# A vision-transformer step pipelined over 128 images: score units in another order, the keys' placement signalled in two halves, and new orders on all engines

## What is computed

```python
h = layernorm(layernorm(patches) @ W + b)          # tok: embedding, PD = 768 -> D = 192
a = layernorm(h)                                    # causal attention, 12 heads of 16
q, k, v = split(a @ w_attn + b_attn)
s = (q*scale) @ k.T + (q*scale) @ rel.T             # relative term by key position
h = h + softmax(where(causal, s, -inf)) @ v @ w_proj + b_proj
hid = layernorm(h); n = layernorm(hid)*g1 + b1      # routed block: 29 tokens of 196
score = sigmoid(n @ Wr + br); idx = the 29 lowest   # these get full attention, 12 heads
merged = where(idx, attention(n) @ Wo + bo, (n + score*pooled) @ Wm + bm)
h3 = hid + merged
out = h + h3 + gelu(layernorm(h3) @ W1 + bf1) @ W2 + bf2
```

## Time and profile before

| what | value |
|---|---|
| time, median of 3 runs | 4944.79 us (4944.5 to 4948.51) |
| the profiled execution's own time | 4944.02 us |
| its span, first to last instruction | 4942.2 us |
| mean granted TensorE clock | 0.989 of full speed |
| busy share of the span: PE / weight loads / DVE / ACT / POOL | 95 / 87 / 78 / 70 / 62 % |

### The profile page before, as it was taken

One profiled execution on the slowest core, in us unless ns is written; L12 is line 12 of the kernel. 1 busy time (PEld: TensorE's weight loads), 2 busy tenths in 40 slices (PEclk: granted clock), 3 DMA queues, 4 the chain that ended last, 5 costly groups with the idle time before them and its releaser, 6 DMA issues. The chain is left out here.

```text
span 4942.2 us, 143405 instructions
## 1 busy us (share of the span) xinstructions
PE 4696.2 (95%) x44376; PEld 4299.3 (87%) x44376; DVE 3872.3 (78%) x13015; ACT 3448.9 (70%) x12030; POOL 3065.9 (62%) x4143
## 2 busy tenths in 40 slices
PE   3899999999999999999999999999999999999998
PEld 3788888888888888888888888888888888888887
DVE  3787887887888788788788878878878877887885
ACT  1667777776776777777677677777777767767775
POOL 2566666666666666666666666666666666666664
PEclk7899999999999999999999999999999999999999
DMA  5555555455555555555555555555554555555551
GB/s 70 68 68 72 69 71 72 66 74 67 69 73 67 72 70 70 72 67 73 69 67 74 67 70 72 68 72 69 71 71 66 74 67 69 72 67 72 70 70 21
DMA packets 339085, 340.16 MB, mean 69 GB/s; under 512 B 47652, under 2 KB 306033, under 8 KB 339057
## 3 DMA queue, kind: packets, MB, share of 16 engines
q1 hardware_dynamic: 332522, 337.37, 52.3%
q10 hardware_dynamic: 6535, 2.45, 0.3%
HBM read 204.78 MB, written 19.27 MB: 45 GB/s over the span
## 5 line engine op out<-in xcount | busy, mean ns | idle before, releaser
L1610 ACT ACTIVATE p<-banks,negmax 98x98 f32<-98x98 f32 (+1 forms) x3072 | 1139.3, 379 | 216.9 <-issue 121.8
L544 POOL TENSOR_TENSOR p<-p,rden 98x392 f32<-98x392 f32 x1152 | 980.9, 870 | 280.8 <-DVE rden L1242 280.7
L1226 DVE TENSOR_REDUCE negmax<-banks 98x2 f32<-98x392 f32 (+1 forms) x1152 | 609.6, 557 | 141.0 <-PE banks L732 122.2
L732 PE MATMUL banks<-kz,qparts 128*98 128x392 f32 x2304 | 648.9, 385 | 0.0
L1610 ACT ACTIVATION_READ_ACCUMULATOR p<-banks,negmax 98x1 f32 x3072 | 612.0, 199 | 0.0
L743 PE MATMUL banks<-tokw,x_sb 128*98 128x193 f32 x3072 | 592.4, 336 | 15.5 <-POOLq L556 14.6
L743 PEld LDWEIGHTS banks<-tokw,x_sb 128*98 128x98 f32 x3072 | 553.9, 252 | 20.3 <-issue 14.6
L767 PE MATMUL banks<-ident,p 98*98 98x98 f32 x4608 | 530.4, 252 | 24.1 <-ACTq L1614 4.1
L695 PE MATMUL banks<-z3Ts,w_split 128*128 128x196 f32 x3840 | 508.4, 279 | 33.7 <-ACT gT L1685 32.3
L695 PEld LDWEIGHTS banks<-z3Ts,w_split 128*128 128x128 f32 x3840 | 468.2, 192 | 64.2 <-ACT gT L1685 58.0
L535 POOL TENSOR_TENSOR gparts<-gT,gparts 128x392 fp32r<-128x392 f32 x384 | 395.2, 1040 | 190.9 <-DVE gparts L1434 190.9
(11 more groups left out here) (264 smaller groups left out, 11542.3 us busy)
## 6 DMA issues: line engine op xcount, KB each, us to landing
x_sb<-in_x SPq DMA_DIRECT2D x384, 196.0 KB, 5.0
kz<-kq SPq DMA_DIRECT2D x1024, 73.5 KB, 2.6
x_sb<-in_x SPq DMA_DIRECT2D x256, 190.8 KB, 8.9
x_sb<-in_x SPq DMA_DIRECT2D x256, 185.5 KB, 11.1
qparts<-kq SPq DMA_DIRECT2D x256, 147.0 KB, 2.7
x_sb<-in_x SPq DMA_DIRECT2D x128, 189.0 KB, 7.3
out<-out_row SPq DMA_DIRECT2D x128, 147.0 KB
pT<-in_L_ffn_W ACTq DMA_DIRECT2D x1, 576.0 KB
```

Source lines behind the costliest of these rows:

```text
L544: gp.tensor_tensor(heads, heads, rden[:, g, t, s0:s0 + sn].unsqueeze(2).broadcast_to([HT, sn, w]), ALU.mult).then_inc(sem["pnorm_sb"], 1)
L732: last = mm(o, qparts[:, g, HT * t:HT * t + HT], kz[:, slots[0]:slots[-1] + 1, part, g, 0:w], start=False, stop=part == 1, skip_group_chec ...
L1226: ve.tensor_reduce(negmax[:, g, t, slots[0]:slots[-1] + 1], bank[RING[f"S{k}"]][0:HT, 0:w * len(slots)].rearrange("p (s w) -> p s w", w=w) ...
L1610: sc.activation((p1 if t else p0)[0:HT, 4 * g + s], bank[b][0:HT, w * i:w * i + w], ACT.Exp, bias=negmax[:, g, t, s:s + 1], accum_out=den[ ...
```

## The change

1. `s_unit`: in each group the unit of the last rows' heads 0 and 1 is scored first, then the one of all four heads' first rows, then that of heads 2 and 3. Each unit's work is the same as before.
2. `place_keys`: the two `qparts` copies are issued first; the eight `kz` copies are signalled by two semaphores, `kza_in` (slots 0 and 1) and `kzb_in` (slots 2 and 3). S0 waits for `q_in` and `kza_in`, S1 for `kzb_in`.
3. The lists of `step` on PE, DVE, ACT and POOL are ordered anew. No instruction is added or dropped, except that the changed lists split or join waits.

The core of the diff, with hunks of the same kind left out ("..."):

```diff
-    g, part = divmod(u, 3)
+    g, j = divmod(u, 3)
+    part = (1, 0, 2)[j]
...
                 sp.wait_ge(sem["kqlo_sb"], after("kqlo_sb", n))
+                for part in range(2):
+                    sp.dma_start(qparts[64 * part:64 * part + 64].bitcast(F32),
+                                 kq[64:128, part].bitcast(F32)).then_inc(sem["q_in"], 16)
...
-                                         sem["kz_in"], 16)
-                for part in range(2):
-                    sp.dma_start(qparts[64 * part:64 * part + 64].bitcast(F32),
-                                 kq[64:128, part].bitcast(F32)).then_inc(sem["q_in"], 16)
+                                         sem["kza_in" if s < 2 else "kzb_in"], 16)
...
-                            pe.wait_ge(sem["kz_in"], after("kz_in", n))
+                            pe.wait_ge(sem["kza_in"], after("kza_in", n))
+                        if k == 1:
+                            pe.wait_ge(sem["kzb_in"], after("kzb_in", n))
```

More of the change, by code:

```diff
@@ L67 @@
 SEMS = dict(
-    x_in=len(XROWS) * 16, out_done=16, kz_in=8 * 16, q_in=2 * 16,
+    x_in=len(XROWS) * 16, out_done=16, kza_in=4 * 16, kzb_in=4 * 16, q_in=2 * 16,
     tok_mm=1, sqs_mm=1, zT_mm=1, score_mm=1, mrow_mm=1, usum_mm=1, kk_mm=1, vv_mm=1, aT_mm=1, kq_mm=1, v_mm=1,
@@ L593, in step @@
                 if front:
[L594 to L597, removed]
                     normalised(8)
+                if back:
+                    gp.drain()
+                    gp.tensor_tensor(h2b[:], h2[:], both(bf2), ALU.add).then_inc(sem["h2b_sb"], 1)
                 if head:
@@ L619, in step @@
                         sem["f_rstd"], 1)
+                if tail:
+                    gelu_low(2)
+                if back:
+                    gp.wait_ge(sem["h3_stat"], after("h3_stat", m))
+                    rstd(mv_3[:, :, 1], ve5[:], rstd5[:], "h3_rstd")
                 if back:
@@ L992, in step @@
                 if back:
+                    score()
                     keys2()
[L994 to L999, removed]
                 if front:
                     causal("S0")
+                if back:
+                    values2()
+                    mixing_rows()
+                if front:
                     causal("S1")
@@ L1051, in step @@
                     up(2)
+                if front:
+                    attention()
+                if head:
+                    attention_cols()
                 if back:
                     attn_out()
-                if head:
-                    attention_cols()
-                if front:
-                    attention()
-                if back:
-                    scatter()
                 if front:
@@ L1063, in step @@
                     keys()
+                if back:
+                    scatter()
                 if tail:
@@ L1464, in step @@
                     sigmoid()
+                if front:
+                    maxima(0)
+                if back:
                     mixing_rows()
                 if front:
-                    maxima(0)
                     maxima(1)
-                    maxima(2)
-                if tail:
-                    mlp_cols_lo()
-                if front:
-                    maxima(3)
                 if back:
@@ L1477, in step @@
                     inverse_sums(0)
-                    inverse_sums(1)
+                    maxima(2)
+                    maxima(3)
                 if back:
@@ L1481, in step @@
                 if front:
-                    inverse_sums(2)
+                    inverse_sums(1)
                     maxima(4)
                     maxima(5)
+                if back:
+                    q_blocks()
+                if front:
+                    inverse_sums(2)
+                if tail:
+                    mlp_cols_lo()
+                if front:
                     inverse_sums(3)
@@ L1487, in step @@
                 if back:
-                    q_blocks()
+                    max2()
+                if front:
+                    inverse_sums(4)
+                    maxima(7)
+                    inverse_sums(5)
                 if head:
@@ L1502, in step @@
                 if front:
-                    maxima(8)
+                    transposed("A0")
                     inverse_sums(6)
-                    transposed("A0")
                 if head:
-                    embedding_scaled()
+                    embedding()
                 if front:
@@ L1521, in step @@
                     attention_input()
+                if front:
+                    attention()
+                if head:
+                    attention_cols_lo()
                 if tail:
@@ L1524, in step @@
                     gelu_parts(1)
+                if front:
+                    residual()
                 if back:
                     attn_out()
[L1527 to L1528 removed]
                 if tail:
                     gelu_parts(2)
[L1531 to L1532 removed]
+                if head:
+                    keys()
                 if back:
@@ L1692, in step @@
                     values()
+                if tail:
+                    mlp_cols_hi()
+                if front:
                     load_table(ACT.Exp)
@@ L1721, in step @@
                     softmax(8)
+                if tail:
+                    load_table(ACT.Gelu)
+                if front:
                     transposed("A1")
@@ L1727, in step @@
                 if tail:
-                    load_table(ACT.Gelu)
                     gelu(0)
```

86 lines of the change are left out of this document (31 added, 55 removed).

## The result

The changed kernel takes 4861.7 us (median of 3 runs, 4861.03 to 4862.09) against 4944.79 us: 83 us less. The ratio of the runs is 0.983, with a 95% interval of 0.9807 to 0.9852. The forecast was 4830 (4775 to 4900), faster.

A forecast was written before the change was run, and what follows sets the result against it. PE bounds the kernel, with 2.30 us of waits in each 37.40 us body. 25.0+11.3 gave 36.3, 37.40-2.30+1.58 gave 36.68; 36.5 was taken, saving 112 over 124 bodies and about 3 elsewhere: 4830 us (4775 to 4900).

The forecast's parts named there:

- (b): On PE, A1 and B0 take 1.07 where eight transposes need 0.70: 0.37 us of waiting per body.
- (c): On PE, A2 and A3 up to `context2` take 1.15 for 0.70: 0.45 us of waiting per body.
- (d): On PE, B1, A4, A5, B2 and the wait of up(2) take 2.11 for 1.40: 0.71 us per body.
- (e): On PE, `scatter` to `projection` takes 0.83 where 0.36 is needed: 0.47 us of waiting behind DVE's yparts.
- new wait of 0.35 for qb: PE could reach `scores2` before the routed block's queries are ready: 0.35 us of new waiting per body.
- h1b and h2b on POOL: These moved POOL operations lie beside work of other engines and were priced at nothing.
- the 6.84 of the sum: On PE, up(2), attention, attention_cols, attn_out, projection and keys together take 6.84 us at full pace.
- late a_row: Rival, chance 0.18: POOL products hold `embedding_scaled` and the h1 write, 0.3 each; period 37.0, 4895 us.
- those 2.30 us: Five listed waits inside PE per body, the only source of gain besides smaller waits.
- Slower: Rival, chance 0.08: DVE operations held up beside POOL make `ao` 1.3 later; period 37.8, 4995 us.
- No difference: Rival, chance 0.04: ACT's chain starts no earlier, since nTs comes as much later as S0 earlier; 4945 us.
- Better: Rival, chance 0.10: `ao` and gelu_low(2) find DVE and POOL earlier; period 35.9, 4760 us.

The follow-up runs named there:

- e2b: Changed kernel with `place_keys` as before: eight `kz` copies, then `qparts`, one semaphore that S0 waits for; 5301.4 us, ratio 1.0717.
- e11: Kernel before with the changed lists of all four engines from up(2) on; 5014.0 us, ratio 1.0131 to the kernel before.
- e3b: Changed kernel with POOL's h2b moved back ahead of `normalised(0)`; 4833.2 us, ratio 0.9769 to the kernel before.
- e9: Changed kernel with all four lists as before from up(2) on; 5144.7 us, ratio 1.0399 to the kernel before.
- e1b: Kernel before with the new unit order and the key placement in two halves, all lists as before; 5034.6 us, ratio 1.0173.
- e8: Kernel before with only the new key placement, old unit order, S0 waiting for both new semaphores; 4948.7 us, ratio 1.0001.
- e4b: Changed kernel with embed(0) back between `keys2` and S0 on PE; 5143.3 us, ratio 1.0391 to the kernel before.
- e10: Changed kernel with POOL's h2b moved behind `normalised(5)`; 4852.0 us, ratio 0.9811 to the kernel before.

## Why the prediction was right, and where it was not

**Right: what bounds, and where the gain sits.** Waits (b), (c), (d) and (e) are gone, S0 stands at P+3.45 without a wait for a copy, and the chain starts 2.3 earlier. e2b shows that the new placement carries this: without it S0 waits 2.2, where the prediction said 3.

**Sizes in the first two thirds.** First exponential: P+6.34, under the 6.6 to 7.0. The third, smaller wait of ACT (0.35) went as well, and each wait that went gave 0.1 more than the idle shown, since successive rows of ACT overlap by that (the copy of vv ends at 2507.49, the exponential starts at 2507.40). The new wait of 0.35 for qb did not come: `scores2` starts at P+13.17. The prediction let qs end 6.00 after the first exponential "with the same content"; in the new unit order one dear unit stands ahead of qs and not two, and qs ends 5.50 after it (2512.90). up(2) starts at P+24.50 instead of 25.0.

**The step that failed: "h1b and h2b on POOL ... I cost them at nothing".** The tail took 12.27 from up(2) instead of 11.3. Of the 0.97, 0.65 is the wait for a_row, 0.19 is work that the 6.84 of the sum had too short, 0.08 more stands at `scatter` (0.64 for 0.56) and 0.04 more in `down` (0.29 for 0.25). The 0.19 is no wait: up(2) takes 1.27 up to `attention`, the same two groups take 1.29 in e11 (2522.32 to 2523.61), and up(1) takes 1.18. The 0.65 is the rival "late a_row" (0.18): its mechanism came in full, while the earlier up(2) paid for most of it. I had named `embedding_scaled` and the h1 write. The first takes 0.86 in the changed kernel and 0.75 before, the second 2.06 and 1.32, and e3b shows the cause: with h2b away from it, it takes 1.22 and nothing waits for a_row. And wkeep, which reads 98x2 elements, takes 836 ns in e3b beside an operation of POOL of 840. By the Trainium skill (SBUF — State Buffer, Who interferes with whom), of a DVE instruction with two SBUF inputs and a GpSimd instruction that reads SBUF the second one waits for the end of the first. The trace of e3b agrees: wkeep, started 0.02 behind `normalised(0)`, ends at 2531.13 and `normalised(0)` at 2531.12.

**"A gain can come only out of those 2.30 us" held, but the parts do not add.** The prediction priced head and tail each by itself: -1.5 and +0.45 or so. The tail alone did about what was priced (e11, +66 us). The head alone did not (e9, +196 us): it needs a list behind it that has work where ctxT and a_row are late and that writes kq_lo early enough for the copies. And the unit order was costed at nothing, but costs 86 us under the old lists (e1b less e8). In the new lists it is what lets S0 start on the first half of the `kz` copies; what it costs or gives there no run shows by itself.

**The rivals.** "Slower" needed `ao` 1.3 later than forecast; the wait for it is 0.64 against 0.56. "No difference" needed ACT's chain to start as late as before; it starts 2.3 earlier. "Better" needed `ao` and gelu_low(2) to be early; both waits came.

**The signs.** The prediction says of itself that it is wrong if `attention_cols` waits for a_row, and that wait came. It also wanted PE busy for over 96% of the span (95% measured). The others came: no wait for a copy, `projection` without a wait, one at `scatter` and one in `down`.

**The range.** 4862 lies inside 4775 to 4900 and inside the forecast's own 4792 to 4870, above the 4830. The body is 36.77 against 36.5 forecast and the sum of the terms, 36.3: the 0.2 kept in reserve was right in kind and too small. There is luck in it: up(2) came 0.5 earlier than forecast and the tail took 0.97 longer, so two errors of opposite sign cancel by half.

## What to carry to other kernels

Price a change of order as a whole list: take each engine's queue at full pace, and ask at each place what covers the next operand that is late. A part that looks like the gain can be a loss without the part that looks like a cost. Where DVE and POOL both read SBUF, write their lists side by side; moving one POOL operation shifts the hold to another DVE line, so look at its neighbours' durations before and after. And a wait on TensorE can cost more than its length: those of 1.5 us (e4b) and 2.2 us (e2b) per body cost 1.5 and 1.6 times as much here, since the granted clock fell behind them. But e9's wait of 1.67 per body cost hardly more than itself (0.23 of clock per body by the means), so the length alone does not tell.

## What the runs showed of the hardware

The granted clock: in e4b, where PE waits 1.5 us once per body, the 3 us behind the wait are granted 0.62 in the body shown, between the levels of 1.2 and 2.4 GHz, and the mean over the run is 0.971; with a wait of 2.2 (e2b) it is 0.958. It does not fall behind every such wait: between 3000 and 3400 us it falls in five of some ten bodies in e4b, in eight of some nine in e2b, and in one of ten in e9, whose wait of 1.67 is longer than e4b's. What decides between them no run shows. With three waits of 0.3 to 0.65 per body (the changed kernel) the mean is 0.989, and all that is missing lies at the ends of the run: from 300 to 4650 us 1.00 is granted. I had expected the wait alone.

The hold between DVE and POOL does not depend on the size of DVE's operation: 160 to 732 ns for msq on 98x2, 221 to 836 ns for wkeep (medians), 405 ns to 1241 ns for a half of h1 (the least, and the one beside h2b in the body shown). It lasts about as long as POOL's operation still runs: msq in e10 starts at 2544.32 and takes 0.74, and h2b beside it ends at 2545.04.
